# Feed-forward for each node's two experts alone: node rows scattered to expert regions and computed in blocks of 128

## The reference

```python
xn = _layernorm(x)
# graph: mean over the incoming edges' sources, then a linear layer, relu, row norm
neigh_mean = segment_sum(xn[src], dst) / max(deg, 1)
g = normalize(relu(concat([xn, neigh_mean]) @ W + b))
# mix: q, k, v = xn @ W_qkv + b_qkv; centred and squared q and k; kv = k2.T @ v
x = x + g + (v + q2 @ kv / sqrt(N)) @ W_out + b_out
# feed-forward: 8 experts, hidden 682, the two most likely per node
probs = softmax(flat @ router_w.T); topk_probs, topk_idx = top_k(probs, 2)
gates = one_hot weights of the two, divided by their sum
h = silu(flat @ w1[e].T) * (flat @ w3[e].T)
x = x + sum_e gates[:, e] * (h @ w2[e].T)
```

## Time and profile before

| what | value |
|---|---|
| time, median of 2 runs | 3562.48 us (3548.16 to 3576.8) |
| span of the profiled execution | 3246.4 us |
| the profiled execution's own time | not given |
| busy PE, DVE, ACT, POOL | 3017.6, 2330.4, 952.3, 1750.2 us |
| DMA | 316.83 MB, mean 98 GB/s |

### The profile page before, as it was taken

How to read it: one execution, slowest core, us unless ns; L and a number is a source line. 1 busy time by engine, 2 the same in 40 slices (tenths; PEclk the granted TensorE clock), 3 DMA queues, 4 the chain that set the end, 5 groups by cost and what they waited for, 6 DMA issues and landing times.

```text
span 3246.4 us, 54000 instructions
## 1 busy us (share of the span) xinstructions
PE 3017.6 (93%) x16013; PEld 1716.1 (53%) x16014; DVE 2330.4 (72%) x6541; ACT 952.3 (29%) x1845; POOL 1750.2 (54%) x1707
## 2 busy tenths in 40 slices
PE   6994566999999999999999999999999999999999
PEld 4773355554554554554555545545545545555444
DVE  6466666776776777776777767767767767777654
ACT  2345211322222222222222223223222222222333
POOL 1006777664674664764755746746746647656000
PEclk9996688999999999999999999999999999999999
DMA  6342343333333333333333333333333333334000
GB/s 217 118 154 65 98 115 110 111 101 90 102 108 91 100 105 89 108 100 87 108 87 103 105 92 101 103 90 100 109 90 100 103 88 106 101 98 95 26 14 18
DMA packets 159847, 316.83 MB, mean 98 GB/s; under 512 B 47862, under 2 KB 83918, under 8 KB 159566
## 3 DMA queue, kind: packets, MB, share of 16 engines
q0 software_dynamic: 83424, 235.38, 25.4%
q1 hardware_dynamic: 76142, 77.92, 8.3%
HBM read 293.72 MB, written 19.45 MB: 96 GB/s over the span
## 4 chain that ended last, share of the span: by engine, by line
PE 87%; issue 5%; POOL 3%; DVE 3%; DMA 1%; ACT 1%; DVEq 1%; POOLq 0%; ACTq 0%
PE bank L830 14%; PE bank L831 14%; PE bank L832 14%; PE bank L816 7%; PE bank L818 6%; PE bank L817 6%; PE bank L670 5%; PE bank L672 5%; POOL rows L495 3%; PE bank L773 3%; PE bank L779 2%; PE bank L709 2%; PE bank L720 2%; PE bank L724 1%; PE bank L764 1%
## 5 line engine op out<-in xcount | busy, mean ns | idle before, releaser
L495 POOL DMA_INDIRECT rows<-xn_split,srcw x1666 | 1734.2, 1041 | 994.9 <-PE bank L672 535.7
L830 PE MATMUL bank<-x2a,wts 128*128 128x512 f16 (+1 forms) x2236 | 826.8, 372 | 46.6 <-issue 44.4
L831 PE MATMUL bank<-x2a,wts 128*128 128x512 f16 (+1 forms) x2236 | 826.6, 372 | 0.0
L832 PE MATMUL bank<-x2a,wts 128*128 128x512 f16 (+1 forms) x2236 | 826.2, 372 | 0.0
L633 ACT ACTIVATE hh<-hid 128x512 f16<-128x512 f32 (+1 forms) x559 | 338.2, 605 | 1645.5 <-DVE hid L1289 1645.5
L1279 DVE SCALAR_TENSOR_TENSOR hid<-bank,cst,sig 128x512 f32<-128x512 f32 (+1 forms) x559 | 401.2, 718 | 385.0 <-PE bank L832 278.5
L670 PE MATMUL bank<-rows,hot 128*128 128x256 f16 x1666 | 413.1, 283 | 107.6 <-DMA rows<-xn_split,srcw 81.0
L629 ACT ACTIVATE sig<-bank,cst 128x512 f32<-128x512 f32 (+1 forms) x559 | 365.2, 653 | 294.2 <-PE bank L832 292.1
L816 PE MATMUL bank<-hh,wts 128*128 128x512 f16 (+1 forms) x1118 | 411.1, 369 | 19.2 <-DVE hh L1260 17.9
L672 PE MATMUL bank<-rows,hot 128*128 128x257 f16 x1666 | 415.1, 283 | 0.0
L818 PE MATMUL bank<-hh,wts 128*128 128x512 f16 (+1 forms) x1118 | 410.8, 369 | 0.0
(11 more groups left out here) (260 smaller groups left out, 2672.9 us busy)
## 6 DMA issues: line engine op xcount, KB each, us to landing
rows<-xn_split,srcw POOLq DMA_INDIRECT x1666
gate<-gates_t SPq DMA_DIRECT2D x96, 256.0 KB
wts<-in_wT POOLq DMA_DIRECT2D x24, 688.0 KB, 4.5
xt<-in_x SPq DMA_DIRECT2D x49, 128.0 KB
xnt<-xn_cols SPq DMA_DIRECT2D x49, 128.0 KB
xn_cols<-rows SPq DMA_DIRECT2D x12, 512.0 KB, 6.2
gate<-gates_t SPq DMA_DIRECT2D x72, 84.0 KB
out_t<-x1a SPq DMA_DIRECT2D x22, 256.0 KB, 3.7
```

The costliest lines, as they stand in the source:

```text
L495: pool.indirect_dma_start(rows[:, g * WG + m, 0:2 * C], None, XH, bass.IndirectOffsetOnAxis(ap=srcw[:, par, e:e + 1], axis=0))\
L830: pe.matmul(o, whi, xhi, start=(c == 0), stop=False)
L831: pe.matmul(o, whi, xlo, start=False, stop=False)
L832: last = pe.matmul(o, wlo, xhi, start=False, stop=(c == KC - 1))
```

## The change

The feed-forward is taken out of the node loop. The program now has these parts, one after the other:

- The first pass as before, with buffers at fixed addresses in one arena, and eight small extra stores of padding.
- The sums of tiles 0 to 3. Between their 36 groups 25 chunks of weights are loaded by SP, split by ScalarE and VectorE, and stored by SP in HBM (`WD`), laid out by expert. Three experts are loaded back while the node groups run, the other five after them.
- `node_groups`: 13 groups of up to four tiles. A group has 36 steps; in them it sums the neighbours of the next four tiles, and in steps 0 to 14 it updates its own four tiles together, each operation over four tiles where the layout allows. The value part of the attention is a product of its own, and the query is normalized after the product with `mix` instead of before. The router takes exp from ScalarE. Ranks within each expert come from two small matmuls with a triangular matrix and with ones; a row with features (high and low), gates and node number, 1088 bytes, is scattered by POOL to the region of each of its two experts (`scatter`, two indirect DMAs a tile), and SP stores the updated node rows to `ACC`.
- After the last group VectorE works out from the counts which expert and which rows each of 105 blocks has (`expi`, `rowi`), and SP pads the regions' ends.
- `blocks`: 105 blocks of 128 rows, four in a loop turn. Rows are loaded, transposed and stand still in TensorE while the expert's weights stream (`wexp` at an expert number held in a register): 24 matmuls of 384 or 298 columns. The hidden values, in f32, are transposed, split, and 18 matmuls of 256 columns give the result with nodes in partitions. VectorE multiplies by the gate, and POOL adds the rows to `ACC` with an accumulating indirect DMA, each waiting for the one before.
- The sums are loaded from `ACC`, transposed, and stored in the output's layout, 13 groups.

The core of the diff:

```diff
+REGION = -(-NODES // P) * P + P
+BLOCKS = (2 * NODES + EXP * (P - 1)) // P
+RING = 4
+STEPS = BT * GROUPS
...
+        def node_groups(engine, body):
+            with engine.Fori(0, (FULL_GROUPS - 2) // 2) as turn:
+                for par in range(2):
+                    body(2 * turn + par, par, STEPS, STEPS)
...
+        def blocks(engine, body):
+            for k in range(RING):
+                body(k, k)
+            with engine.Fori(1, BLOCKS // RING) as turn:
+                for k in range(RING):
+                    body(RING * turn + k, k)
...
+            def scatter(g, par):
+                pool.wait_ge(s_slot, g + 1)
+                pool.sem_inc(s_pool, 1)
+                for q in range(tiles_in(g)):
+                    rows_ = LAST if isinstance(g, int) and BT * g + q == TILES - 1 else P
+                    for k in range(2):
+                        pool.indirect_dma_start(XD, bass.IndirectOffsetOnAxis(ap=sloti[0:rows_, par, k, q:q + 1], axis=0),
+                                                xrow[0:rows_, par, q, :].bitcast(I32), None).then_inc(s_scat[par], 16)
...
+            for t in range(BT):
+                gather_tile(t, t % 2, t // 2 + 1)
+            def node_group(g, par, sums, steps):
+                for q in range(sums // GROUPS):
+                    if q == 2:
+                        scatter(g, par)
+                    gather_tile(BT * (g + 1) + q, q % 2, 2 * (g + 1) + q // 2 + 1)
...
+            def block_(i, k):
+                pool.wait_ge(s_y, i + 1)
+                if some(i):
+                    pool.sem_inc(s_pool, 1)
+                    pool.wait_ge(s_acc, 16 * i)
+                pool.sem_inc(s_pool, 1)
+                pool.indirect_dma_start(ACC, bass.IndirectOffsetOnAxis(ap=xb[:, k, ID_AT:ID_AT + 2].bitcast(I32), axis=0),
+                                        yb[:, k % 2, :], None, compute_op=ALU.add).then_inc(s_acc, 16)
...
+            def first(i, k, a, e):
+                o, m = (0, HALF) if a == 0 else (HALF, HID)
+                if some(i):
+                    pe.wait_ge(s_hid[a], i)
+                turns = [(j, h) for j in range(2 * KC) for h in ((0, 1) if j < KC else (0,))]
+                for n, (j, h) in enumerate(turns):
+                    for w, H in enumerate((H1, H3)):
+                        f = first_weight(w, j % KC, h, o)
+                        last = pe.matmul(H[a][:, 0:m - o], xbt[:, k % 2, j * P:(j + 1) * P],
+                                         wexp[:, ds(e, 1), f:f + m - o].rearrange("p e j -> p (e j)"),
+                                         start=(n == 0), stop=(n == len(turns) - 1))
+                last.then_inc(s_h[a], 1)
...
+            def block_(i, k):
+                if not some(i):
+                    turn_input(0, 0)
+                e = expert(i)
+                pe.wait_ge(s_ready, e + 1)
+                pe.wait_ge(s_xt, i + 1)
+                first(i, k, 0, e)
+                if some(i):
+                    turn_hidden(i - 1, 1)
+                if not (isinstance(i, int) and i == BLOCKS - 1):
+                    turn_input(i + 1, k + 1)
+                first(i, k, 1, e)
+                turn_hidden(i, 0)
+                if some(i):
+                    second(i - 1, k - 1, expert(i - 1))
...
-            def ffn_block(b, summed, tiles, cols):
-                pe.wait_ge(s_x2, b + 1)
-                for j in range(HT):
...
-                    if j >= 2:
-                        second(b, j - 2, cols)
-                    for q, i in GROUP_AT[j]:
-                        if q in summed:
-                            sum_group(BT * b + 2 + q, i)
-                    for q, s in stages_at(j, tiles):
-                        update(BT * b + 1 + q, (q + 1) % 2, s)
```

More of the change, by code:

```diff
@@ L52 @@
 RSQRT_MAGIC = float(0x5F3759DF)
[L58 to L80, removed]
+REGION = -(-NODES // P) * P + P
+BLOCKS = (2 * NODES + EXP * (P - 1)) // P
+SPARE = BLOCKS - -(-2 * NODES // P)
+XROWS = EXP * REGION + SPARE * P
+XROW = 544
+GATES_AT, ID_AT = 2 * C, 2 * C + 2 * EXP
+HALF = 3 * P
+KT = FULL + 1
+W1W3 = 2 * KC * 2 * HID
+WEXP = W1W3 + 2 * KT * C
+CHUNKS = 2 * KC * EXP // 2 + EXP + 1
+STORED = 2
+RING = 4
+STEPS = BT * GROUPS
 def some(n):
@@ L96, in rows_count, with rest_pieces, chunk_dmas, chunk_count @@
     return 16 * sum(map(group_size, mine)) * t + 16 * sum(group_size(k) for k in mine if k <= i)
[L99 to L107, removed]
-    return out
+def rest_pieces(e):
+    out, r, end = [], e * REST, (e + 1) * REST
+    while r < end:
+        n = min(P - r % P, end - r)
+        out.append((r - e * REST, n, HT_FULL + r // P, r % P))
+        r += n
+    return out
+def chunk_dmas(c):
+    if c < 2 * KC * EXP // 2:
+        return 2
+    if c < CHUNKS - 1:
+        return 1
+    return sum(len(rest_pieces(e)) for e in range(EXP))
+def chunk_count(c):
+    return 16 * sum(chunk_dmas(k) for k in range(c + 1) if k % 4 == c % 4)
+def chunk_weight(c):
+    return c // EXP if c < 2 * EXP else 2
+def tiles_in(g):
+    return BT if not isinstance(g, int) else min(BT, TILES - BT * g)
 def gnn_mix_moe(nc, x, srcT, dstT, dst_rows, Wg, bg, Wq, Wk, WvT, bq, bk, bv, Wo, bo, rwT, wT, outT):
     with ExitStack() as ctx:
-        def sb(name, shape, dt=F32):
-            return ctx.enter_context(nc.sbuf_tensor(name, shape, dt))
         def sem(name):
@@ L844, in _, with half @@
[L844 to L849 removed]
+            for q in range(BT):
+                for i in range(GROUPS):
+                    sum_group(q, i)
+            pe.wait_ge(s_mix, 1)
+            def half(q):
+                return slice((q % 2) * C, (q % 2) * C + C)
@@ new lines, in turn_hidden, with second @@
+            def turn_hidden(i, a):
+                pe.wait_ge(s_hid[a], i + 1)
+                if some(i):
+                    pe.wait_ge(s_lo[a], i)
+                for j in range(3):
+                    last = pe.transpose(HTP[a][:, j * P:(j + 1) * P], hid[:, (3 * a + j) * P:(3 * a + j + 1) * P], ident[:, :])
+                last.then_inc(s_htp[a], 1)
+            def second(i, k, e):
+                for a in range(2):
+                    pe.wait_ge(s_lo[a], i + 1)
+                if some(i):
+                    pe.wait_ge(s_y, i)
+                for j in range(KT):
+                    rows_ = P if j < FULL else REST
+                    for n, (h, w) in enumerate(((0, 0), (0, 1), (1, 0))):
+                        f = last_weight(w, j)
+                        last = pe.matmul(YP[:, 0:C], hh[0:rows_, k % 2, h, j, :],
+                                         wexp[0:rows_, ds(e, 1), f:f + C].rearrange("p e j -> p (e j)"),
+                                         start=(j == 0 and n == 0), stop=(j == KT - 1 and n == 2))
+                last.then_inc(s_yp, 1)
@@ L1305, in _ @@
[L1305 to L1318 removed]
+            window(0, 0)
```

1283 lines of the change are left out of this document (768 added, 515 removed).

## The result

The changed kernel takes 3743.95 us (3733.3 to 3754.59, two runs) against 3562.48: a ratio of 1.051, 95% interval 1.039 to 1.064. The forecast was 3914 with a range of 3700 to 4250 and 0.90 on slower. Sign and range held; the median came out 170 us under the forecast.

What follows compares the result with a forecast made beforehand. The prediction took TensorE to bound the kernel before, its expert matmuls (about 2000 us) laid over POOL's 2193 us of gathers. With that overlap lost, terms summed to a 3598 us span, plus 316 gave 3914; range 3700 to 4250.

Steps and rivals of the forecast that it cites:

- Steps 2 to 5: First to last gather: first four tiles 215 us, other 45 tiles 1958, 96 scatters 123, TensorE stalls in node groups 36.
- Step 1: First pass over the nodes, same engines and order as before, up to the first gather: 262 us.
- Step 6: Last gather to first block: last tile's chain, table of blocks, eight padding stores and first load, 75 us.
- Step 7: The 105 blocks at 6.7 us each, 704 us, plus 25 loop turns at 6 us, 150 us.
- Step 8: End: 13 groups loaded, transposed and stored at 235 GB/s, plus first load, last store and handshakes, 75 us.
- I keep that 316: Timed median 3562.5 us lay 316 us above the profiled span; the same 316 was added to the predicted span 3598.
- rival A: The whole kernel as summed, its longest term POOL's counted gather queue: 3914 us, own range 3780 to 4080; chance 0.60.
- Rival C: Gather stage dearer, with scatters and TensorE stalls at their upper bounds: 211 us more, 4125; chance 0.14.
- Rival B: Blocks bound by something else than matmuls, such as accumulating scatters waiting for each other: 357 us more, 4270; chance 0.17.
- Rival D: POOL's gather step shrinks to 0.95 us because issue overlaps with descriptors: 581 us less, 3333; chance 0.04.
- Rival E: The 316 us outside the span belong to the old program and vanish: about 3600, no change; chance 0.05.
- TensorE sets the end: Kernel before: TensorE, busy 93% and 87% of the chain that ended last, was the bound, with POOL near second.

Runs made afterwards that it cites:

- e9: The changed kernel itself, unaltered, run again beside the kernel before at 3234.1 us: 3466.7 us, ratio 1.071.
- e7: The changed kernel with six one-hot buffers made four groups ahead, scatters spread, ScalarE's expert-weight loads after the first block loads: 3714.3 us, ratio 1.056.
- e1: The changed kernel with 16 extra unused products on TensorE after each of a tile's first eight sum groups: 3478.4 us, ratio 1.075.
- e4: The changed kernel with all low parts left out of the blocks, 8 instead of 24 and 6 instead of 18 matmuls: 3324.2 us, ratio 1.03.
- e10: The kernel before with one product of three kept in its expert feed-forward: 3158.3 us beside 3234.1, ratio 0.975.
- e8: The kernel before itself, unaltered, run for a profile: 3233.6 us, span 3231.9.
- e6: The kernel before with one product of three kept in its expert feed-forward: 3346.2 us beside 3518.8.

## Why the prediction was right, and where it was off

Against e9, the level of the profile that was read:

| term | predicted | e9 | 
|---|---|---|
| 1 first pass | 262 | 237 |
| 2 first four tiles | 215 | 210 |
| 3, 4, 5 other tiles, scatters, stalls | 1958 + 123 + 36 = 2117 | 2122 |
| 6 last gather to first block | 75 | 95 |
| 7 blocks | 704 + 150 = 854 | 761 |
| 8 end | 75 | 44 |
| span | 3598 | 3470 |

- **Steps 2 to 5 held.** The last gather was to come near 2600 and came at 2570 us (2830 at the slower level). A scatter took 1.04 + 0.30 us in e9, TensorE's stalls 23 us for the 36 of the text, and what is left for 1530 gathers is (2122 - 96 x 1.34 - 23) / 1530 = 1.29 us, taken as 1.28: the nearest row was the right price. VectorE's one-hots lengthen gathers: in e9 those beside a one-hot alone took 1.26 us (median of 243), those beside no VectorE operation 0.95 (1004). 250 of the 1530 took over 1.0 us. One of them:

```profile
985.14 0.69 DVE L1387 TENSOR_TENSOR hot<-lane,dstf 128x512 f16<-128x512 f16 x1 [4.63 <-PE bank L938]
985.38 1.27 POOL L693 DMA_INDIRECT rows<-xn_split,srcw  x1 [0.30 <-PE bank L938]
```

  The Trainium skill's page "SBUF — State Buffer", section "SBUF: two separate sides", says that a VectorE operation with two inputs in SBUF (the on-chip memory) holds, when it starts first, the port pair that it shares with GpSimd for its whole length, against a GpSimd operation that reads SBUF. The trace fits that: the one-hot reads two tiles in SBUF, the gather its row numbers there, and the 0.32 us more lie within the 0.45 us that the one-hot still had to run.
- **Step 1** was read from one run. Over the changed kernels the first gather came at 227 to 263 us, with POOL waiting for VectorE's maxima: up to 35 us of scatter in a term taken as fixed.
- **Step 6** left out a queue. Eight padding stores of 136 KB were counted as issues; ScalarE starts five loads of 2.1 MB at the same moment, and the first block load waits for the stores. SP in e9:

```profile
2629.35 8.11 SPq L593 DMA_DIRECT2D routed<-padrow  x8
2661.63 3.67 SPq L604 DMA_DIRECT2D xb<-routed  x4
```

  24 us lie between the two. e7, where the weights come later, took 75.7 us, the number of the text.
- **Step 7, the loop turn, is the term that was mis-sized most.** Starts of a block's first products in the changed kernel, five blocks around one turn of the loop:

```profile
3299.75 2.12 PE L1122 MATMUL bank<-wexp,xbt 128*128 x12 [0.73 <-issue]
...
3306.73 2.12 PE L1122 MATMUL bank<-wexp,xbt 128*128 x12 [0.31 <-issue]
...
3313.85 2.12 PE L1122 MATMUL bank<-wexp,xbt 128*128 x12 [0.33 <-issue]
...
3320.75 2.12 PE L1122 MATMUL bank<-wexp,xbt 128*128 x12 [0.31 <-issue]
...
3328.29 1.96 PE L1122 MATMUL bank<-wexp,xbt 128*128 x11 [0.74 <-issue]
```

  A turn costs some 0.4 us more than the step between two blocks inside the body, where the earlier trace rows had 4.96 and a slow start after it; the clock stays at the higher level. Of the 150 us some 10 came. The text had named the lower bound, "a loop that short might be held", and did not take it. A block inside the loop steps by 7.0 to 7.2 us on average, against 6.7: 105 x 0.4 = 40 us too little there, against some 140 too much for the turns.
- **Step 8** was 44 us: the last 13 groups moved at 294 GB/s, where 235 was taken, a rate that no row of before shows.
- **"I keep that 316" failed as reasoning.** Nothing lies outside the span: time and span differ by 2 us or less (3733.3 and 3731.7). The profile of before came from the faster level (3246), the timed runs from the slower (3562). What must be carried over is the price of that level for the changed kernel, 3720 to 3744 less 3467 = 253 to 277 us; 254 of the 262 us between the two spans lie in the gather stage (2376 against 2122 in the windows). 3598 + 316 was 128 too high in the first part and 39 to 63 in the second.
- **The range held partly by luck.** 3744 is under rival A's own range (3780 to 4080), and inside the stated one because the timed runs fell at the slower level. At the faster level, from which every row was read, the kernel takes 3467 us, under the range's 3700, and is 233 us slower than the kernel before, where 352 were forecast. The sign does not hang on it: the kernel is slower by 5 to 7% at both levels.
- **Rival C** has the right place for the slower level (late waits at the gathers, last gather 236 us later than forecast, priced at 211), but not by its cause: the granted clock of that stage is 0.58 at both levels, and at the faster one e1 raised it to 0.84 for 15 us. Added to the 316 it would have counted the same time twice. **Rival B** is refuted by 566 us of waiting for yb in the accumulations' row; a step that did wait for the landing before it took 4.6 us in e4, under the 7.1 of a block. The landing of an accumulation, 3.8 us, is more than the 2.3 that were worked out from the Trainium skill, page "DMA: Bandwidth & Descriptors", section "Anatomy of one DMA — SWDGE (gpsimd) path"; the measurement decides. **Rival D** is refuted by [0.30 <-issue] throughout. **Rival E** named the right quantity and the wrong way for it to go: it did not vanish, since the changed kernel has its gathers too.
- **"TensorE sets the end" was only half of it.** The chain of waits showed it truly, but e10 shows that the next bound stood 76 us behind. Freed of the dense feed-forward altogether, the node groups fell to POOL's bound: gathers begin to end from 2726 (e8, 248.7 to 2974.3) to 2333 us in e9, 393 less. After the last gather stand 900 us instead of 258. 642 lost and 393 gained, with an 11 us earlier first gather, give the 238 us between the spans of e8 and e9.

The lost cover accounts for the loss. e1 put 6272 idle products, 608 us more of TensorE's busy time, under the gathers and took 3478 us where e9 took 3467; the blocks are 711 us of such time and stand alone. That blocks run while gathers still do was not tried: each expert's weights would have to be in SBUF beside the gathers' buffers.

## What to carry to other kernels

Work removed from an engine that overlaps with another's queue is worth what the next bound leaves, so thin it out in place and time that before counting on the sum; and price what loses its cover at its full length. A constant taken as the difference between a profile's span and the timed runs is no overhead until one run shows both. When large transfers start beside small ones that something waits for, price the small ones behind the large.

## What the runs showed of the hardware

- A batch of runs can be one in which semaphore increments come up to several us late (in the pair of timelines above VectorE saw a finished sum 5.5 us later), on all engines, while POOL issues indirect gathers and not while it issues accumulating scatters. It costs 6 to 10% in the three kernels that ran at both levels (e6 over e10 1.06, the changed kernel 1.07 to 1.08, the kernel before 1.09 to 1.10), and the blocks, a stage without gathers, take the same 761 us at both.
- An accumulating scatter of 128 rows of 1 KB took 1.55 us on POOL where a plain one took 1.0, and landed after 3.8 us; one that waited for the landing before it started 4.6 us after that one (e4). Beside 10.7 MB of weight loads the first landed after more than 12 us (e7).
- A loop whose body is four blocks (some 210 matmuls) turned at 0.4 us; one with a whole group of nodes and a dense feed-forward turned at 5 us. What decides between them was not tried.
- With a granted clock of 0.58 between first and last gather (e9) the gather stage takes 2333 us, with 0.84 (e1) 2318. e1 also gives TensorE 582 us more to do there, so a gain by the clock and a loss by that work may offset each other; only their sum, 15 us, is shown.
